# A four-layer graph network on one core: the same scales without a power, one column scalar per factorisation step, residual adds in pairs

## The reference, cut to what matters

```python
h = jnp.maximum(_layernorm(x), 0.0); x = x + _L0_gnn_ref(h, adj, ...)   # spectral: U relu(U' h W1 + b1) W2 + b2
h = jnp.maximum(_layernorm(x), 0.0); x = x + _L1_gnn_ref(h, adj, ...)   # Linear, batch norm, relu, Linear, batch norm
h = jnp.maximum(_layernorm(x), 0.0); x = x + _L2_gnn_ref(h, adj, ...)   # two graph convolutions, then four LSTMs
h = jnp.maximum(_layernorm(x), 0.0); x = x + _L3_gnn_ref(h, W, adj)     # attention with four heads
return x

def _layernorm(x, axis=-1, eps=1e-05):
    m = jnp.mean(x, axis=axis, keepdims=True)
    v = jnp.var(x, axis=axis, keepdims=True)
    return (x - m) / jnp.sqrt(v + eps)
```

## Time and profile before

| | |
|---|---|
| median of 3 runs | 1466.67 us (1466.48 to 1467.83) |
| the profiled execution | 1467.47 us, span 1465.7 us |
| PE busy | 1049.7 us, 72% |
| DVE busy | 990.5 us, 68% |
| ACT busy | 733.8 us, 50% |
| POOL busy | 364.4 us, 25% |
| chain that ended last, by engine | PE 55%, DVE 28%, issue 7%, ACT 4%, POOL 3% |
| granted TensorE clock, mean | 0.937 |

### The profile page before, as it was taken

One profiled execution on the slowest core, in us unless ns is written; L12 is line 12 of the kernel. 1 busy time (PEld: TensorE's weight loads), 2 busy tenths in 40 slices (PEclk: granted clock), 3 DMA queues, 4 the chain that ended last, 5 costly groups with the idle time before them and its releaser, 6 DMA issues.

```text
span 1465.7 us, 22119 instructions
## 1 busy us (share of the span) xinstructions
PE 1049.7 (72%) x5403; PEld 636.9 (43%) x5403; DVE 990.5 (68%) x3973; ACT 733.8 (50%) x2047; POOL 364.4 (25%) x1138
## 2 busy tenths in 40 slices
PE   3666666666442350288877488999999998489997
PEld 1444444455321130255533366444445443356665
DVE  8777888888879999856767543444343454667776
ACT  2333444444242436144745375866454555377775
POOL 4044556566347551003100400000020030310000
PEclk9999999999999995599988599999999999589999
DMA  5000000000100000000000000000000000000011
GB/s 148 1 1 1 1 1 1 1 2 1 31 23 1 1 0 1 1 0 0 0 0 0 0 0 0 0 0 0 1 0 0 1 0 0 0 9 27 23 29 30
DMA packets 16658, 12.34 MB, mean 8 GB/s; under 512 B 665, under 2 KB 14530, under 8 KB 16578
## 3 DMA queue, kind: packets, MB, share of 16 engines
q1 hardware_dynamic: 16578, 11.49, 2.8%
HBM read 7.23 MB, written 4.19 MB: 8 GB/s over the span
## 4 chain that ended last, share of the span: by engine, by line
PE 55%; DVE 28%; issue 7%; ACT 4%; POOL 3%; DMA 1%; DVEq 1%; ACTq 0%; POOLq 0%
PE P L1404 31%; PE P L716 13%; DVE arena L371 2%; DVE arena L491 2%; PE P L1546 2%; POOL nt L955 2%; DVE arena L550 2%; DVE arena L552 2%; DVE arena L496 1%; DVE bst_all L933 1%; ACT hb L1202 1%; DVE bcol L390 1%; DVE arena L489 1%; PE P L1539 1%; PE P L1517 1%
## 5 line engine op out<-in xcount | busy, mean ns | idle before, releaser
L1404 PE MATMUL P<-arena,WT 128*128 (+2 forms) x792 | 329.2, 580 | 3.9 <-ACT L1295 2.9
L1404 PEld LDWEIGHTS P<-arena,WT 128*128 128x128 f32 x792 | 151.9, 192 | 181.2 <-issue 167.3
L1308 ACT ACTIVATE arena<-P,bl 128x512 f32<-128x512 f32 (+1 forms) x252 | 153.6, 636 | 139.2 <-PE P L1404 131.8
L716 PE MATMUL P<-arena 1*128 1x127 f32 (+62 forms) x504 | 150.8, 428 | 89.3 <-DVE arena L371 87.1
L716 PEld LDWEIGHTS P<-arena 1*128 1x128 f32 x504 | 122.1, 308 | 131.3 <-DVE arena L368 120.5
L655 ACT ACTIVATE arena<-arena 1x127 f32<-1x127 f32 (+62 forms) x126 | 32.2, 256 | 165.8 <-DVE arena L382 155.5
L1116 DVE TENSOR_TENSOR arena<-arena 128x512 f32<-128x512 f32 (+1 forms) x36 | 22.0, 610 | 137.7 <-ACT arena L1308 137.7
L922 POOL COPY arena<-arena 128x512 f32<-128x512 f32 x16 | 21.2, 1368 | 334.7 <-DVE arena L1127 242.9
L1202 ACT ACTIVATE hb<-xN,nmr,rsd 128x128 f32 (+1 forms) x192 | 78.5, 481 | 51.5 <-PE P L1404 30.8
L203 POOL TENSOR_SCALAR lf<-lf 1x1 f32<-1x1 f32 x210 | 86.3, 411 | 21.9
L716 PE MATMUL P<-arena,Ib 128*128 128x46 bf16 (+1 forms) x318 | 35.5, 273 | 64.0 <-ACT arena L685 63.4
(11 more groups left out here) (500 smaller groups left out, 2606.7 us busy)
## 6 DMA issues: line engine op xcount, KB each, us to landing
out_dram<-xN SPq DMA_DIRECT2D x16, 256.0 KB, 2.3
Wn<-in_L_gnn_Wih_dram SPq DMA_DIRECT2D x4, 256.0 KB, 2.9
Wn<-in_L_gnn_Whh_dram SPq DMA_DIRECT2D x4, 256.0 KB, 2.8
Wqkv<-in_L_gnn_W_dram SPq DMA_DIRECT2D x1, 192.0 KB
W1n<-in_L_gnn_W_dram SPq DMA_DIRECT2D x1, 128.0 KB
W2n<-in_L_gnn_W_dram SPq DMA_DIRECT2D x1, 128.0 KB
Wg<-in_L_gnn_Wg_dram SPq DMA_DIRECT2D x2, 64.0 KB
adj<-in_adj_dram SPq DMA_DIRECT2D x1, 64.0 KB, 1.8
```

The lines of the kernel that those rows point to most:

```text
L716: def mm(o,l,r,start=True,stop=True): return t.matmul(o,lhsT=l,rhs=r,start=start,stop=stop)
L1308: act(s.gt[u][gate][:,0:cols],P[4*u+gate][:,0:cols],f,bias=s.bl[:,4*(p-1)+gate:4*(p-1)+gate+1]).then_inc(ev('lstm_gates'),1)
L1404: def mm(o,l,r,start=True,stop=True,**k): return t.matmul(o,lhsT=l,rhs=r,start=start,stop=stop,**k)
```

## The change

Five things change.

- In the factorisation, `neg_off2` and `G` are both read as tensors and only the reciprocal as a column scalar (`scalar_tensor_tensor` for `tensor_scalar`).
- In `gpsimd_scales` the power is gone. POOL raises `layer_variance`, ACT takes a square root of it (`layer_roots`), DVE makes the reciprocal (`layer_inverse`), and POOL goes on with its Newton step. Both new pieces have a fixed place in their engine's order. The multiplication of `a` by -0.5 moves ahead of the wait.
- In the loops at the ends of the second and third layers, both adds of a pair come ahead of both groups' statistics.
- `bn_final` replaces two of its steps around the reciprocals by a Newton step of the inverse root, and takes minus the mean while ACT makes the root.
- In the stage behind it ACT signals `hb` and `yb` apart, and PE waits for each just ahead of its use.

```diff
-            f=c.mark(ts(D_down[:,i:i+1],neg_off2[:,i:i+1],inv_down[:,i-1:i],G[:,i:i+1],ALU.mult,ALU.add))
+            f=c.mark(stt(D_down[:,i:i+1],neg_off2[:,i:i+1],inv_down[:,i-1:i],G[:,i:i+1],ALU.mult,ALU.add))
             c.wait(b)
-            b=c.mark(ts(D_up[:,j:j+1],neg_off2[:,j+1:j+2],inv_up[:,j+1:j+2],G[:,j:j+1],ALU.mult,ALU.add))
+            b=c.mark(stt(D_up[:,j:j+1],neg_off2[:,j+1:j+2],inv_up[:,j+1:j+2],G[:,j:j+1],ALU.mult,ALU.add))
...
-    e(tt(cc,cc,d,ALU.add))
-    e(tt(b_,cc,s.neghalf[:,0:1].broadcast_to([N,l-f]),ALU.pow))
+    tt(cc,cc,d,ALU.add).then_inc(ev('layer_variance'),1)
+    e.mark(ts(a,a,-0.5,None,ALU.mult))
+    eng.wait_ge(ev('layer_variance'),2*k-2+(first>0))
+    eng.wait_ge(ev('layer_inverse'),2*k-3+(first>0))
     e(tt(d,b_,b_,ALU.mult))
     e(tt(d,d,cc,ALU.mult))
     e(ts(d,d,-0.5,1.5,ALU.mult,ALU.add))
-    e.mark(ts(a,a,-0.5,None,ALU.mult))
     e(tt(rsd,b_,d,ALU.mult))
...
     v.tensor_scalar(bn[:,0:nh],var,1e-5,None,ALU.add).then_inc(ev('batch_variance'),1)
+    c.mark(v.tensor_scalar(bn[:,10:10+nh],mean,-1.0,None,ALU.mult))
     v.wait_ge(ev('batch_root'),k)
     c(v.reciprocal(bn[:,4:4+nh],bn[:,2:2+nh]))
-    c(v.tensor_tensor(bn[:,4:4+nh],bn[:,4:4+nh],bn[:,0:nh],ALU.mult))
-    c(v.tensor_tensor(bn[:,4:4+nh],bn[:,4:4+nh],bn[:,2:2+nh],ALU.add))
-    c(v.tensor_scalar(bn[:,4:4+nh],bn[:,4:4+nh],0.5,None,ALU.mult))
-    c(v.reciprocal(bn[:,6:6+nh],bn[:,4:4+nh]))
-    c(v.tensor_tensor(s.bsc[:,col:col+nh],bn[:,6:6+nh],gamma,ALU.mult))
-    c(v.tensor_tensor(bn[:,8:8+nh],mean,s.bsc[:,col:col+nh],ALU.mult))
-    v.tensor_tensor(s.bsh[:,col:col+nh],beta,bn[:,8:8+nh],ALU.subtract).then_inc(ev('batch_scale'),1)
+    square=c.mark(v.tensor_tensor(bn[:,6:6+nh],bn[:,4:4+nh],bn[:,4:4+nh],ALU.mult))
+    c.mark(v.tensor_tensor(bn[:,8:8+nh],bn[:,4:4+nh],gamma,ALU.mult))
+    c.wait(square)
+    c(v.scalar_tensor_tensor(bn[:,6:6+nh],bn[:,6:6+nh],-0.5,bn[:,0:nh],ALU.mult,ALU.mult))
+    c(v.scalar_tensor_tensor(s.bsc[:,col:col+nh],bn[:,6:6+nh],1.5,bn[:,8:8+nh],ALU.add,ALU.mult))
+    c(v.tensor_tensor(bn[:,12:12+nh],bn[:,10:10+nh],s.bsc[:,col:col+nh],ALU.mult))
+    v.tensor_tensor(s.bsh[:,col:col+nh],beta,bn[:,12:12+nh],ALU.add).then_inc(ev('batch_scale'),1)
...
+  def layer_inverse(s,v,k,portion):
+    f,l=((0,GB*FIRST_GROUPS),(GB*FIRST_GROUPS,NB))[portion]
+    root=s.nt[:,NB+f:NB+l]
+    v.wait_ge(s.ev('layer_root'),2*k-2+portion)
+    v.reciprocal(root,root).then_inc(s.ev('layer_inverse'),1)
...
     with v.Fori(0,NP-1) as it: residual_a(it,True)
+    s.layer_inverse(v,2,0)
     residual_a(NP-1,False)
...
     with v.Fori(0,NP-1) as it:
-        for u in range(2):
-            residual(0,it,u)
-            residual_stats(0,it,u)
+        for u in range(2): residual(0,it,u)
+        for u in range(2): residual_stats(0,it,u)
+    s.layer_inverse(v,3,0)
     for u in range(2): residual(0,NP-1,u)
...
+    s.layer_inverse(v,4,0)
     for u in range(2): residual(NG+2,NP-1,u)
     s.vector_hT(v,0,1)
     for u in range(2): residual_stats(NG+2,NP-1,u)
...
+  def layer_roots(s,a,k,portion):
+    f,l=((0,GB*FIRST_GROUPS),(GB*FIRST_GROUPS,NB))[portion]
+    a.wait_ge(s.ev('layer_variance'),2*k-2+portion)
+    a.activation(s.nt[:,NB+f:NB+l],s.nt[:,2*NB+f:2*NB+l],ACT.Sqrt).then_inc(s.ev('layer_root'),1)
...
     relu_a(NP-1,False)
     a.sem_inc(ev('expand_hidden_first'),2)
+    s.layer_roots(a,2,0)
     s.first_scales(a,2)
...
-            act(s.hb[u][:,:],R1[:,bass.ds(g*C,C)],ACT.Relu,bias=s.bsh[:,0:1],scale=s.bsc[:,0:1])
+            act(s.hb[u][:,:],R1[:,bass.ds(g*C,C)],ACT.Relu,bias=s.bsh[:,0:1],scale=s.bsc[:,0:1]).then_inc(ev('contract_hidden'),1)
             act(s.yb[u][:,:],R1[:,bass.ds(8192+g*C,C)],ACT.Relu,bias=s.bsh[:,1:2],scale=s.bsc[:,1:2]).then_inc(ev('contract_hidden'),1)
...
+    s.layer_roots(a,4,0)
     s.first_scales(a,4)
     s.scalar_h(a,0,0)
     s.scalar_h(a,1,1)
+    s.layer_roots(a,4,1)
     a.preload_act_table(ACT.Exp)
     s.scalar_qkv(a,0,0)
...
-            t.wait_ge(ev('contract_hidden'),2*it+u+1)
             t.wait_ge(ev('contract_out'),2*it+u+1)
+            t.wait_ge(ev('contract_hidden'),4*it+2*u+1)
             mm(P[u][:,:],s.W2T[:,0,:],s.hb[u][:,:],stop=False)
+            t.wait_ge(ev('contract_hidden'),4*it+2*u+2)
             mm(P[u][:,:],s.W2T[:,1,:],s.yb[u][:,:],start=False).then_inc(ev('contract_product'),1)
```

More of the change, by code:

```diff
@@ L77, in build @@
     xcol=sb("xcol",[N,1])
-    neghalf=sb("neghalf",[N,1])
     bcol=sb("bcol",[N,1])
@@ L183, in _ @@
         c.mark(eng.memset(lf[:,:],0.0))
-        c.mark(eng.memset(neghalf[:,:],-0.5))
         c.wait(c.n)
@@ L288, in _ @@
         tt(gap[:,:],gap[:,:],near[:,:],ALU.add).then_inc(ev('eigen_from_gpsimd'),1)
-        net.gpsimd_chain,net.neghalf=e,neghalf
+        net.gpsimd_chain=e
         for first,last in ((0,FIRST_GROUPS),(FIRST_GROUPS,NG)): net.gpsimd_scales(eng,2,first,last)
@@ L1059, in hidden_b @@
             v.bn_stats(s.bst2[:,bass.ds(g*6,6)],R1[:,bass.ds(g*C,C)]).then_inc(ev('batch_stats'),1)
-    with v.Fori(0,NP-1) as it: hidden_b(it,True)
+    with v.Fori(0,2) as it: hidden_b(it,True)
+    s.layer_inverse(v,2,1)
+    with v.Fori(2,NP-1) as it: hidden_b(it,True)
     hidden_b(NP-1,False)
@@ L1099, in vector @@
     layer_e(0,True)
-    with v.Fori(1,NP) as it: layer_e(it,False)
+    layer_e(1,False)
+    s.layer_inverse(v,3,1)
+    with v.Fori(2,NP) as it: layer_e(it,False)
     v.sem_inc(ev('lstm_hidden'),2)
@@ L1130, in vector @@
     with v.Fori(0,NP-1) as it:
-        for u in range(2):
-            residual(NG+2,it,u)
-            residual_stats(NG+2,it,u)
+        for u in range(2): residual(NG+2,it,u)
+        for u in range(2): residual_stats(NG+2,it,u)
+    s.layer_inverse(v,4,0)
     for u in range(2): residual(NG+2,NP-1,u)
@@ L1140, in vector @@
     s.vector_hT(v,1,1)
+    s.layer_inverse(v,4,1)
     s.vector_round(v,-1,1)
@@ L1255, in scalar_main @@
     s.act_ln(a,0,'expand_')
-    with a.Fori(0,4) as it: hidden_b(it,True)
+    hidden_b(0,True)
+    s.layer_roots(a,2,1)
+    with a.Fori(1,5) as it: hidden_b(it,True)
     s.last_scales(a,2)
-    with a.Fori(4,NP-1) as it: hidden_b(it,True)
+    with a.Fori(5,NP-1) as it: hidden_b(it,True)
     hidden_b(NP-1,False)
@@ L1276, in scalar_main @@
             act(s.zb[u][:,:],R2[:,bass.ds(g*C,C)],ACT.Identity,bias=s.bsh[:,2:3],scale=s.bsc[:,2:3]).then_inc(ev('residual_mixed'),1)
+    s.layer_roots(a,3,0)
     s.first_scales(a,3)
@@ L1290, in scalar_main @@
     s.act_ln(a,0,'conv_')
-    with a.Fori(0,4) as it: layer_e(it,True)
+    layer_e(0,True)
+    s.layer_roots(a,3,1)
+    with a.Fori(1,5) as it: layer_e(it,True)
     s.last_scales(a,3)
-    with a.Fori(4,NP-1) as it: layer_e(it,True)
+    with a.Fori(5,NP-1) as it: layer_e(it,True)
     layer_e(NP-1,False)
```

## The result

The changed kernel takes 1431.82 us (median of 4 runs, 1430.70 to 1432.68) where the kernel before, beside it on the chip, takes 1467.25. The ratio is 0.9758, 95% interval 0.9741 to 0.9775: faster. The forecast was 1434.4, range 1428 to 1446. The profiled execution is 1430.7 us, its span 1429.0, so 36.7 us of span are gone. PE is busy for 1043.3 us (73%), DVE for 975.4, ACT for 735.8, POOL for 335.4, and the mean granted clock is 0.946.

A forecast was written before the change was run, and what follows sets the result against it. The chain of waits was on PE for 55% and DVE for 28%, with the LSTMs untouched. Terms summed to -32.3 us, from 1467.47 to 1435.2; less 0.8 for the median below its profiled run, 1434.4 us, range 1428 to 1446.

The forecast's parts named there:

- Factorisation: Twisted factorisation on DVE: 127 steps shrink from 0.56 to 0.45 us, 14.0 us, less 3.0 of waits; net -11.0 us.
- The step's formula: Factorisation, bottom chain: reciprocal 0.162 plus operation 0.209 plus two handovers of 0.04 us sets the step at 0.45 us.
- The waits for POOL: Factorisation: DVE, now quicker, waits for POOL's pieces: 1.2 us, 1.4 for shorter pieces, 0.4 added; 3.0 us in all.
- The rivals of a dearer and of a cheaper operation: Factorisation: new operation costs as much as the old, 1445.5 us (0.12), or as little as a reciprocal, 1430.5 (0.07).
- That POOL becomes the bound: Factorisation's first 53 steps: POOL's reading instructions slow, up to 6 us more, DVE waits; 1440 us, chance 0.06.
- Second layer's end: Statistics to ACT's start takes 5.1 us for 12.6 without the power, -7.5; shorter loop rounds, -2.7; -10.2 us in all.
- 3.67 becomes 3.2 us: Residual loop at second layer's end: pairing adds removes two add-to-statistics handovers per pair, 0.47 us a round over six rounds.
- Third layer's end: Same loop and POOL path as the second layer, -10.1; later Exp table load behind ACT's second root, +1.3; net -8.8 us.
- +1.3 for the second root: Third layer's end: ACT's second root delays the Exp table load, so the copies the scores wait for end 1.3 us later.
- First layer's end: The power was nearly hidden; ACT's root comes only after its last relu, so the longer way costs +0.4 us.
- Batch norms, split signal, second parts: Shorter ACT scale waits, -0.6; PE starting on `hb` without `yb`, -2.3; second parts' roots and reciprocals in paused loops, +0.2 us.
- The clock rival: LSTMs: TensorE's 1.2 GHz level lasts into them; from 33 us of such work the gain is gone; 1475 us, chance 0.02.

The follow-up runs named there:

- experiments 1: Changed kernel with only the factorisation taken back to two column scalars (`tensor_scalar`) in each chain: 1441.19 us, ratio 0.9825 to the kernel before.
- experiment 2: Changed kernel with DVE's pieces of the small iteration set at later steps of the factorisation: 1427.58 us, ratio 0.9724 to the kernel before.
- experiment 6: Changed kernel with the power back on POOL in all six calls, without roots on ACT and reciprocals on DVE: 1443.14 us, ratio 0.9847.
- experiment 5: Kernel before with only the two residual loops paired, the power kept on POOL: 1456.78 us, ratio 0.9933.
- experiment 4: Changed kernel with both residual loops unpaired and written out as seven rounds without a branch: 1433.30 us, ratio 0.9777 to the kernel before.
- experiment 3: Changed kernel with both residual loops unpaired again (add, statistics, add, statistics): 1438.90 us, ratio 0.9813 to the kernel before.
- experiment 8: Changed kernel with the power back on POOL only for the second part (16 columns) ahead of the attention layer: 1429.67 us, ratio 0.9740.
- experiment 7: Changed kernel with ACT's root of the first part moved ahead of the last pair's relus at the first layer's end: 1429.57 us, ratio 0.9744.
- experiment 10: Changed kernel with the signals of `hb` and `yb` joined again, PE waiting for both: 1434.26 us, ratio 0.9780 to the kernel before.

## Why the prediction was right, point by point

**Factorisation** (-11.0; -9.7). The step's formula, reciprocal plus operation plus two handovers, holds: 0.15 + 0.22 + 2 x 0.04 = 0.45 us. The term is mis-sized by 1.4: experiments 1 and 2 give 12.6 us, not 14.0. The median step fell from 0.561 to 0.458 us, so the new one is some 0.01 longer than the forecast's 0.45, which is about 0.9 us over 127; the rest lies in the steps with or beside a piece. The waits for POOL, 3.0 in the forecast, were 2.95 by experiment 2, with another split: the long one took 1.51 us, where the forecast wrote 1.2 though its own 10.2 less 9.3 is 0.9, the three short ones 1.1 (1.4 forecast for four). The rivals of a dearer and of a cheaper operation fall with 215 ns. That POOL becomes the bound falls with 352 ns for 331: of the contention that the Trainium skill states for DVE instructions with two SBUF inputs (GPSIMD Engine Reference, section 1, Specifications) this trace shows 6% in this group, for DVE instructions of one column. Single groups of two POOL instructions got up to 22% longer, and most didn't change.

**Second layer's end** (-10.2; -12.8). The path is right: 7.5 predicted for the power, 7.6 by experiment 6. The loop's gain is the mis-sized term: 2.7 predicted, 5.0 by experiment 5. The step that failed is "3.67 becomes 3.2 us": it counted two handovers from add to statistics (0.50) and took the rest of the round as fixed. The loop-back had a share of 0.41 us, 0.21 of it only in this loop of the kernel before, and pairing hid all of it. Even the 0.50 was not all a wait for the add: 0.28 were register instructions (experiment 4). The Trainium skill (Advanced Engine Details and Errata, Control Flow Timing) gives about 108 ns for a compare-and-branch. In the unpaired loops the next add was 0.21 and 0.42 us late, which is register instructions and the branch together, and in the paired loop it was 0; so the figure of the branch alone doesn't give a round's loss. The reciprocal of 48 columns took 0.45 us where "some 0.2" was taken, and DVE was free when the root came: the two errors nearly cancel.

**Third layer's end** (-8.8; -10.3). The same two: 7.0 for the power, and 4.3 for the loop by experiment 3. The forecast took the second layer's round of 3.67 us for this loop too, but its own was 3.46, so pairing saved 0.72 us a round here and not 0.93. Of the +1.3 for the second root, 1.1 came, but only 0.5 of it is the root and the table: without them, the later rise of the clock would have cost the other 0.6 (experiment 8).

**First layer's end** (+0.4; +0.6). As predicted, with the reciprocal's 0.46 as the difference; experiment 6 gives the same 0.6 and experiment 7 shows that it was the place of the root.

**Batch norms, split signal, second parts** (-0.6, -2.3, +0.2; -0.8, -2.5, none seen). ACT waits 1.46 us for the first batch norm's scale, where the earlier trace rows had 1.86. A pair behind it takes 3.44, as predicted; experiment 10 gives 2.9 for the split, 2.6 of it without the clock. Of the -2.5, 0.4 are the clock's too, by the same price: the low stretch ended 7.6 us behind the first `hb` before and 6.8 after. The split's own share is then -2.1 for -2.3.

**What the forecast did not have**: -2.0 ahead of the factorisation, and +1.3 at the LSTM start. They nearly cancel, which is luck, and neither is made by an edit near them. The forecast's sum was -32.3 and the profiles differ by -36.7. The 4.4 us are the two layer ends (-4.1), the factorisation (+1.3), these two (-0.7), and five small ones (-0.9 together).

**The clock rival** (0.02) was wrong in size and right in place: in the profile of after the lower level reaches 3.4 us further into the LSTMs' start than before, not 33. Other executions had less of it than before, so it is not shown to be the change's.

## What to carry to other kernels

A loop's round on an engine holds sequencer time (register instructions, the branch) that counted here when the engine's queue was nearly empty (0.47 to 0.68 us a round) and was free when several instructions were queued. Put the instructions that need no new wait last in the round, and look at the start of the next one: here 0.19 us behind the last statistics meant that it was hidden, 0.40 and 0.61 that it wasn't. Look at each loop by itself, even when the code is the same: the third layer's had a shorter round than the second's. When an instruction on a neighbour takes over a long one, look at what stands ahead of it in that neighbour's order (the last relu: 1.7 us), and when DVE becomes quicker, move the pieces that wait for a slower engine (3.0 us).
